# Neuron scan with gated FFN, one core: unread matmuls of block 0 behind the coupling, first weight quarter in three transfers, three low-half parts moved

## The chip, the cores and the metric

One core of one Trainium2 chip runs the whole program. The metric is the device time of one execution in microseconds (us). The engines are named as in the profile: PE is TensorE (PEld its weight loads), DVE VectorE, ACT ScalarE, POOL GpSimd, SP SyncE, which issues most DMAs.

## The reference, cut to what matters

A scan of 128 time steps (T) over 16 batch rows and 256 neurons, each step four Runge-Kutta stages, and on its output a gated mixture-of-experts FFN. Each Runge-Kutta stage needs the one before it.

```python
def _derivative(q, p, drive, coupling, bias):
    i_couple = jnp.tanh(q) @ coupling.T
    dq = q - q ** 3 / 3.0 - p + drive + i_couple + bias
    dp = EPSILON * (q + ALPHA - BETA * p)
# _rk4_step: four derivatives, q and p advanced and clipped; 128 steps in sequence
logits = x @ W_router.T              # x: the q trace, (2048, 256)
sh = _silu_and_mul(x @ Ws_gate_up, I_SH) @ Ws_down
gu = jnp.einsum('th,ehi->eti', x, We_gate_up)      # 8 experts of 176, top 2
out = x0 + shared_out + sparse_out
```

## The kernel before, in words

**Blocks and stages.** The 128 time steps are 16 blocks of 8 steps; a step has 4 stages, so a block has 32 stages (`STAGES`), and the stage number n runs from 0 to 511 over the scan. Block b's FFN is spread over the stages of blocks b+1 and b+2 by tables with one entry per stage. Block 0 (n = 0 to 31) therefore has no FFN work; in it the FFN's weights are prepared instead. After the last block a tail finishes the FFN.

**One stage of the scan.** DVE writes the new q (L907). ACT computes its tanh twice, to f16 (`th_hi`, L475) and to f32 in PSUM (`th_ps`, L476). DVE subtracts them (`th_lo`, L875). PE's `couple` does three 32-column matmuls on the input (L597), eight 16-column matmuls of `th_hi` with the coupling matrix (L613) and four of `th_lo` (L619), all summed in `coup_ps`. DVE then forms the next q from `coup_ps` and its own cubic term (L907).

**What sets the order.** Every engine has one queue in program order, and the orders are written out by hand. On PE a stage is `couple`, then `prepare(n)`, then the `ffn` work of that stage. On DVE the FFN work and the preparation of a stage (`slot`, `prepare`) stand ahead of `th_lo` where the stage is the first of a time step (k = 0), and behind the `force` operation of L886 otherwise.

**Preparing the up weights (block 0 and the start of block 1).** w_up is four quarters of 2112 columns (1056 KB each). In stages n = 1 to 12 ACT sums absolute values of one third of a quarter per stage (L445, 704 columns; part p in stage p + 1), waiting for the quarter's transfer (`in_w`, L444 and after). In stages 13 to 16 these sums become a power-of-two scale: PE turns the column (L543, stage 13) and spreads the maximum (L547, stage 14), each between two DVE steps. From stage 16 on, each of 17 tiles of 4 rows is split in a high f16 half (ACT, `HI_AT`, L453) and a low half. The low half is made in one of three ways: by DVE (`LO_AT`, L830), by POOL in two operations (`POOL_SCALE_AT` L1024, `POOL_LO_AT` L1032), or by PE as two matmuls into a PSUM bank that is free then (`REST_AT`, L577 with an f32 identity, L578), which ACT rounds (`ROUND_AT`, L457). `REST_AT` has two parts in each of stages 18, 19, 22 to 31 and 33, and its first entry is stage 18; tile 4's parts use `up_ps[0]`, in stages 26 and 27.

**Unread matmuls.** In stages 17 to 34 PE also runs matmuls of 128 columns whose result nobody reads (L601). Their number is that of the table `WARM` at n - 1: ten in stages 17, 18, 21 and 22, two in stage 33, none elsewhere (42 in all). They stand inside `couple`, behind the three matmuls of L597 and ahead of the wait for `th_hi`:

```python
WARM_FROM, WARM_TO = 17, STAGES + 3
WARM = [max(0, 10 - 5 * len(REST_AT.get(n, ())) - 8 * (n == STAGES)) for n in range(WARM_TO)]
```

**Loads.** SP issues, in this order: coupling (256 KB), the first 8 steps of x (128 KB), the identity (64 KB), w_up quarters 0 and 1, x steps 8 to 23 (256 KB), w_up quarters 2 and 3, the rest of x, the small constants, w_down (2 MB).

Of the kernel before, what the change touches and what calls it, by code (L numbers as in the profile page):

```python
# [28 lines left out]
P = 128  # L29
# [6 lines left out]
STAGES = 4 * STEPS  # L36
# [36 lines left out]
def err(z):  # L73
# [33 lines left out]
ROWS = 2 * KC  # L107
# [15 lines left out]
            44: ((10, 2, 4),), 47: ((13, 0, 2),), 49: ((13, 2, 4),)}  # L123
REST_BANK = {14: 2, 1: "route", 6: "down", 4: 0, 3: 1, 9: 2, 7: "down", 10: "route", 13: "down"}
LO_AT = {17: (5, 0), 18: (5, 2), 19: (5, 3), 20: (8, 1), 21: (8, 2), 22: (8, 3), 23: (2, 1), 24: (2, 2), 25: (2, 3),
         26: (0, 1), 27: (0, 2), 28: (0, 3), 29: (12, 0), 30: (12, 2), 31: (12, 3), 32: (11, 0), 41: (11, 2),
         45: (11, 3), 48: (15, 0), 49: (15, 3), 52: (16, 1), 55: (16, 2), 56: (16, 3)}
POOL_SCALE_AT = {17: (5, 1), 19: (8, 0), 22: (2, 0), 25: (0, 0), 27: (12, 1), 30: (11, 1), 37: (15, 2), 39: (15, 1),
                 45: (16, 0)}
POOL_LO_AT = {18: (5, 1), 21: (8, 0), 23: (2, 0), 26: (0, 0), 29: (12, 1), 31: (11, 1), 38: (15, 2), 42: (15, 1),  # L130
              46: (16, 0)}


def in_order(table):
# [31 lines left out]
    return max(rounds_done(tile) for tile in REST_TILES if REST_BANK[tile] == bank)  # L166


WARM_FROM, WARM_TO = 17, STAGES + 3
WARM = [max(0, 10 - 5 * len(REST_AT.get(n, ())) - 8 * (n == STAGES)) for n in range(WARM_TO)]  # L170
W_STEPS = 5
HALF = STEPS // 2
X_AHEAD = {1: (0, 2), 2: (0, 3), 3: (1, "m0"), 5: (1, "m1"), 6: (1, 0), 7: (1, 1), 9: (1, 2), 10: (1, 3),
# [9 lines left out]
def program(nc, x, cond, coupling, bias, w_up, w_down, w_route, identity, spread, iota, e_base, out):  # L183
    ctx = ExitStack()
    with ctx:
# [6 lines left out]
        def sem(name):  # L192
            return ctx.enter_context(nc.semaphore(name))
# [86 lines left out]
        in_x_first = sem("in_x_first")  # L280
        in_x_next = sem("in_x_next")
        in_x = sem("in_x")
        in_w = [sem(f"in_w{i}") for i in range(ROWS)]
        in_wd = sem("in_wd")
        setup_v = sem("setup_v")
        setup_t = sem("setup_t")
# [59 lines left out]
        def blocks(block_of):  # L346

            for b in range(BLOCKS):
                block_of(b)
# [10 lines left out]
        @block.sync  # L360
        def _(sync):
            sync.dma_start(cf[:], coupling).then_inc(in_cf, 16)
            sync.dma_start(xs[:, 0:STEPS], x[:, 0:STEPS]).then_inc(in_x_first, 16)
            sync.dma_start(ident[:], identity).then_inc(in_ident, 16)
            for i in range(ROWS):
                sync.dma_start(wf[:, i // 2, i % 2], w_up[:, i // 2, i % 2]).then_inc(in_w[i], 16)
                if i == 1:
                    sync.dma_start(xs[:, STEPS:3 * STEPS], x[:, STEPS:3 * STEPS]).then_inc(in_x_next, 16)
            sync.dma_start(xs[:, 3 * STEPS:T], x[:, 3 * STEPS:T]).then_inc(in_x, 16)
            sync.dma_start(wr[:], w_route).then_inc(in_const, 16)  # L370
            sync.dma_start(iota_s[:], iota).then_inc(in_const, 16)
            sync.dma_start(e_s[:], e_base).then_inc(in_const, 16)
            sync.dma_start(sel[:], spread).then_inc(in_const, 16)
            sync.dma_start(wd[:, 0:TILES - 1, :], w_down[0:(TILES - 1) * P, :].rearrange(
                "(j p) n -> p j n", p=P)).then_inc(in_wd, 16)
            sync.dma_start(wd[0:F % P, TILES - 1, :], w_down[(TILES - 1) * P:F, :]).then_inc(in_wd, 16)

            def store(f):

                sync.wait_ge(out_ready, KC * (f + 1))  # L380
                sync.dma_start(out[:, :, bass.ts(f, TOK)], out_s[:]).then_inc(stored, 16)

            for f in range(BLOCKS):
                store(f)
            sync.wait_ge(stored, 16 * BLOCKS)
# [27 lines left out]
        def _(act):  # L413
# [12 lines left out]
            def prepare(n):  # L426
                if n == 0:

                    nc.scalar.activation(bias_c[:], bias_s[:], ACT.Copy, bias=-SHIFT, scale=1.0).then_inc(setup_a, 1)
                    act.wait_ge(setup_a, 1)  # L430
                    for m in range(KC):
                        bias_x(0, m)

                    act.wait_ge(setup_v, 4)
                    nc.scalar.mul(c16[:, 0, 1], cf[:, 1], scale[:, 0:1]).then_inc(c_cast, 1)
                    act.wait_ge(in_ident, 16)
                    nc.scalar.mul(ident_u[:], ident[:], scale[:, 0:1]).then_inc(unit_cast, 1)

                if SUM_AT <= n < SUM_AT + W_PARTS:

                    part = n - SUM_AT
                    act.wait_ge(in_w[part // 3], 16)
                    if part:
                        act.wait_ge(w_summed, part)  # L444
                    nc.scalar.activation(hidden_flat[:, 0:W_COLS], w_flat[:, bass.ts(part, W_COLS)], ACT.Abs,  # L445
                                         accum_out=w_sum[:, part:part + 1]).then_inc(w_summed, 1)
                if n == MOST_AT:
                    nc.scalar.mul(ident_neg[:], ident[:], -1.0).then_inc(idents_ready, 1)
                for j, r0, r1 in HI_AT.get(n, ()):

                    act.wait_ge(w_scaled, 4)
                    w, w_hi, _ = w_tile(j)
                    nc.scalar.mul(w_hi[:, r0:r1], w[:, r0:r1], scale[:, 1:2]).then_inc(w_hi_ready, 1)  # L453
                for j, r0, r1 in ROUND_AT.get(n, ()):

                    act.wait_ge(w_rest, REST_ORDER.index((j, ROWS - 1)) + 1)
                    nc.scalar.copy(w_tile(j)[2][:, r0:r1],  # L457
                                   rest_bank(j)[:, r0 * P:r1 * P].rearrange("p (r c) -> p r c", r=r1 - r0)
                                   ).then_inc(w_rounded, 1)
                b, st = n // STAGES, n % STAGES  # L460
                for m, at in enumerate(X_AT):
                    if st == at and 2 <= b < BLOCKS - 1:
                        bias_x(b + 1, m)
# [76 lines left out]
        def _(pe):  # L540
# [39 lines left out]
            def couple(b, st):  # L580

                n = b * STAGES + st
                if n == 0:
                    pe.wait_ge(setup_v, 3)
                    pe.wait_ge(unit_cast, 1)
                else:
                    pe.wait_ge(q_ready, n)
                if st % (4 * HALF) == 0:
                    part = 2 + 2 * (st // (4 * HALF))
                    if b < 2:  # L590
                        pe.wait_ge(x_split_ahead, 4 * b + part)
                    else:
                        pe.wait_ge(x_split, 4 * (b - 2) + part)
                t = b * STEPS + st // 4
                at = slice(t, t + 1)
                for x, piece in enumerate((upper(xb, at), upper(x_rest, at), flat(x_low, at))):
                    nc.tensor.matmul(coup_ps[:, 0:CB], ident_u[:], piece, start=x == 0, stop=False,  # L597
                                     skip_group_check=True)
                if WARM_FROM <= n < WARM_TO:
                    for _ in range(WARM[n - 1]):  # L600
                        nc.tensor.matmul(coup_ps[:, 2 * P:3 * P], c16[:, 0, 0, 0:P], c16[:, 0, 0, 0:P],  # L601
                                         start=False, stop=True, skip_group_check=True)

                pe.wait_ge(hi_ready, n + 1)
                if n == 0:
                    pe.wait_ge(setup_v, 6)
                    pe.wait_ge(c_cast, 1)
                for part in range(2):
                    if n == 0 and part:
                        pe.wait_ge(setup_v, 8)  # L610
                    for m in range(KC):
                        for k in range(KC):
                            nc.tensor.matmul(coup_ps[:, m * B:(m + 1) * B], c16[:, part, k, m * P:(m + 1) * P],  # L613
                                             th_hi[:, k, :], start=False, stop=False, skip_group_check=True)

                pe.wait_ge(lo_ready, b * STAGES + st + 1)
                for m in range(KC):
                    for k in range(KC):
                        last = nc.tensor.matmul(coup_ps[:, m * B:(m + 1) * B], c16[:, 0, k, m * P:(m + 1) * P],  # L619
                                                th_lo[:, k, :], start=False, stop=True, skip_group_check=True)  # L620
                last.then_inc(summands, 1)
# [83 lines left out]
            def one_block(b):  # L705
                for st in range(STAGES):
                    couple(b, st)
                    prepare(b * STAGES + st)
                    if b == 1 and st == 0:
                        pe.wait_ge(in_wd, 2 * 16)  # L710
                        pe.wait_ge(in_const, 4 * 16)
                    for f, at in ffn_stages(b, st)[::-1]:
                        ffn(f, at)

            blocks(one_block)
            for f, at in tail_stages():
                ffn(f, at)
# [425 lines left out]
```

## Time and profile before

| what | value |
|---|---|
| median of 3 runs | 653.63 us (652.66, 653.63, 656.25) |
| profiled execution | 656.32 us, of which its span 654.5 us |
| busy in the span | PE 97%, DVE 93%, ACT 55%, POOL 32% |
| chain that ended last | PE 95%, DVE 3%, DMA 1% |
| costliest lines of that chain | L682 29%, L698 22%, L613 17%, L619 15%, L597 6%, L601 1% |
| first and last start of L601 | 28.0 and 54.0 us, 42 matmuls |

The span runs from the first to the last instruction; the execution's own time is 1.82 us longer, for what lies around it. [...] Stage n begins, in what follows, where its first matmul of L597 starts. In the profiled execution stage 2 begins at 8.86 us, stage 17 at 27.93, stage 18 at 29.91, stage 23 at 40.19, stage 27 at 46.67, stage 32 (block 1) at 52.64.

### The profile page before, as it was taken

What the parts mean: (1) busy time and instruction counts of PE and PEld (TensorE: products, weight loads), DVE (VectorE), ACT (ScalarE), POOL (GpSimd) and SP (SyncE); (2) the same over time, 40 slices, a digit from 0 to 9 for tenths busy, and PEclk for the clock granted to TensorE, in tenths of its full rate; (3) what the DMA queues carried; (4) which work ended last, traced back from release to release, by engine and by line L of the source; (5) the groups of instructions that cost most, each with busy time, mean ns of one, the idle gap of its engine ahead of it and who ended that gap; (6) DMA issues with size and microseconds to landing.
All of it is one profiled execution on the core that took longest, in us unless ns stands there. A gap on an engine that the chain in (4) does not pass through costs nothing.

```text
span 654.5 us, 33404 instructions
## 1 busy us (share of the span) xinstructions
PE 637.2 (97%) x12540; PEld 605.6 (93%) x12540; DVE 607.9 (93%) x4517; ACT 359.1 (55%) x1883; POOL 210.3 (32%) x468
## 2 busy tenths in 40 slices
PE   4899999999999999999999999999999999999998
PEld 3699999999999999999999999999999999999997
DVE  7879999999999999999999999999999999999941
ACT  6757655546455554645555564555546455554642
POOL 2214232232423223242322324232232423233253
PEclk9999999999999999999999999999999999999999
DMA  8800000000000000000000000000000000000000
GB/s 331 244 2 3 4 4 11 4 4 11 4 11 4 12 3 4 11 4 12 3 12 3 4 12 3 12 4 12 3 4 12 3 13 3 12 4 3 12 6 15
DMA packets 8786, 13.59 MB, mean 21 GB/s; under 512 B 1168, under 2 KB 7632, under 8 KB 7984
## 3 DMA queue, kind: packets, MB, share of 16 engines
q1 hardware_dynamic: 8336, 11.45, 5.3%
q8 instruction: 98, 1.61, 1.0%
q14 instruction: 64, 0.52, 0.3%
q10 hardware_dynamic: 288, 0.02, 0.0%
HBM read 9.37 MB, written 2.10 MB: 18 GB/s over the span
## 4 chain that ended last, share of the span: by engine, by line
PE 95%; DVE 3%; DMA 1%; ACT 0%; issue 0%; SPq 0%; POOL 0%; DVEq 0%
PE up_ps L682 29%; PE down_ps L698 22%; PE coup_ps L613 17%; PE coup_ps L619 15%; PE coup_ps L597 6%; PE route_ps L657 3%; PE route_ps L636 1%; DMA wf<-in_w_up 1%; PE down_ps L577 1%; PE coup_ps L601 1%; DVE q L907 1%; PE route_ps L577 1%; PE up_ps L577 0%; DVE th_lo L875 0%; DVE w L830 0%
## 5 line engine op out<-in xcount | busy, mean ns | idle before, releaser
L682 PE MATMUL up_ps<-q_hi,w 128*128 128x128 f16 x2176 | 234.8, 218 | 0.2 <-POOL q_lo L1040 0.2
L1077 POOL TENSOR_TENSOR hidden<-hidden,comb_s 128x128 f32<-128x128 f32 x272 | 123.4, 456 | 284.5 <-ACT th_hi L475 278.2
L698 PE MATMUL down_ps<-hidden,wd 128*128 128x128 f32 x1088 | 209.7, 296 | 0.0
L682 PE MATMUL up_ps<-q_lo,w 128*128 128x128 f16 x1088 | 202.8, 218 | 0.0
L475 ACT ACTIVATE th_hi<-q 128x32 f16<-128x32 f32 x384 | 88.0, 229 | 205.4 <-DVE q L907 203.0
L613 PE MATMUL coup_ps<-th_hi,c 128*128 128x16 f16 x4096 | 179.6, 170 | 1.6 <-ACT th_hi L475 0.9
L682 PEld LDWEIGHTS up_ps<-q_hi,w 128*128 128x128 f16 x2176 | 167.6, 97 | 1.0 <-POOL q_lo L1040 0.4
L698 PEld LDWEIGHTS down_ps<-hidden,wd 128*128 128x128 f32 x1088 | 152.9, 191 | 0.0
L613 PEld LDWEIGHTS coup_ps<-th_hi,c 128*128 128x128 f16 x4096 | 139.2, 96 | 9.2 <-ACT th_hi L475 1.0
L619 PE MATMUL coup_ps<-th_lo,c 128*128 128x16 f16 x2048 | 132.7, 173 | 0.3 <-DVE th_lo L875 0.2
L682 PEld LDWEIGHTS up_ps<-q_lo,w 128*128 128x128 f16 x1088 | 105.7, 97 | 0.1
L907 DVE SCALAR_TENSOR_TENSOR q<-coup_ps,c_un,force 128x32 f32<-128x32 f32 x384 | 96.3, 251 | 8.8 <-PE coup_ps L619 5.2
L516 ACT ACTIVATE act_s<-up_ps,unscale 128x128 f32<-128x128 f32 x272 | 97.1, 357 | 8.8 <-PE up_ps L682 8.8
L597 PE MATMUL coup_ps<-xb,ident_u 128*128 128x32 bf16 x512 | 92.7, 181 | 7.9 <-DVE q L907 5.1
L875 DVE TENSOR_TENSOR th_lo<-th_ps,th_hi 128x32 f16<-128x32 f32 x511 | 97.7, 191 | 2.0 <-ACT th_ps L476 1.8
L619 PEld LDWEIGHTS coup_ps<-th_lo,c 128*128 128x128 f16 x2048 | 85.3, 97 | 15.3 <-DVE th_lo L875 0.3
L597 PE MATMUL coup_ps<-x_rest,ident_u 128*128 128x32 bf16 x512 | 90.8, 177 | 0.0
L597 PE MATMUL coup_ps<-x_low,ident_u 128*128 128x32 bf16 x512 | 90.5, 177 | 0.0
L954 DVE TENSOR_TENSOR hidden<-act_s,up_ps 128x128 f32<-128x128 f32 x272 | 76.4, 281 | 13.9 <-ACT act_s L516 13.7
L867 DVE SCALAR_TENSOR_TENSOR square_ps<-q 128x32 f32<-128x32 f32 x384 | 76.8, 200 | 0.0
L871 DVE SCALAR_TENSOR_TENSOR square_ps<-square_ps,q 128x32 f32<-128x32 f32 x384 | 76.4, 199 | 0.0
L739 DVE SCALAR_TENSOR_TENSOR p_sum<-q,p_sum 128x32 f32<-128x32 f32 x384 | 70.8, 184 | 0.0
(122 smaller groups left out, 1060.5 us busy)
## 6 DMA issues: line engine op xcount, KB each, us to landing
wf<-in_w_up SPq DMA_DIRECT2D x4, 1056.0 KB, 10.1
wd<-in_w_down SPq DMA_DIRECT2D x1, 2048.0 KB, 21.2
out<-out_s SPq DMA_DIRECT2D x16, 128.0 KB, 2.2
xs<-in_x SPq DMA_DIRECT2D x1, 1664.0 KB, 18.9
sel<-in_spread SPq DMA_DIRECT2D x1, 408.0 KB, 18.4
cf<-in_coupling SPq DMA_DIRECT2D x1, 256.0 KB, 2.7
xs<-in_x SPq DMA_DIRECT2D x1, 256.0 KB, 9.1
xs<-in_x SPq DMA_DIRECT2D x1, 128.0 KB, 2.7
```

What stands on the lines that cost most here:

```text
L475: nc.scalar.activation(th_hi[:], q[:], ACT.Tanh).then_inc(hi_ready, 1)
L516: nc.scalar.activation(act_s[:, j % 4, :], up_ps[(f * TILES + j) % UPS][:, 0:TOK], ACT.Silu, scale=unscale[:, 1:2]).then_inc(silu_ready, 1)
L597: nc.tensor.matmul(coup_ps[:, 0:CB], ident_u[:], piece, start=x == 0, stop=False, skip_group_check=True)
L613: nc.tensor.matmul(coup_ps[:, m * B:(m + 1) * B], c16[:, part, k, m * P:(m + 1) * P], th_hi[:, k, :], start=False, stop=False, skip_group_ ...
L619: last = nc.tensor.matmul(coup_ps[:, m * B:(m + 1) * B], c16[:, 0, k, m * P:(m + 1) * P], th_lo[:, k, :], start=False, stop=True, skip_gro ...
L682: last = nc.tensor.matmul(up_ps[(f * TILES + j) % UPS][:, h * TOK:(h + 1) * TOK], w16[:, part, k, h, j * P:(j + 1) * P], q[:, k, :], start ...
L698: last = nc.tensor.matmul(down_ps[:, m * TOK:(m + 1) * TOK], wd[:, j, m * P:(m + 1) * P], hidden[:, j, :], start=j == m == 0, stop=j == TI ...
L867: nc.vector.scalar_tensor_tensor(square, q, THIRD[k], q, ALU.mult, ALU.mult).then_inc(squared, 1)
L871: nc.vector.scalar_tensor_tensor(cubic, square, LINEAR[k], q, ALU.subtract, ALU.mult).then_inc(cubed, 1)
L875: nc.vector.tensor_tensor(th_lo[:], th, th_hi[:], ALU.subtract).then_inc(lo_ready, 1)
L907: nc.vector.scalar_tensor_tensor(q_raw[:] if k == 3 else q_in[k + 1][:], coup_ps[:, 0:CB].rearrange("p (m b) -> p m b", m=KC), c_un[:, (0, ...
L1077: nc.gpsimd.tensor_tensor(hidden[:, j, :], hidden[:, j, :], comb_s[:, j, :], ALU.mult).then_inc(weighed, 1)
```

## The change

The loop of unread matmuls leaves `couple` and stands at the end of PE's work of a stage, behind `couple`, `prepare` and `ffn`. It now writes `up_ps[0]` (with start set) in place of a spare part of `coup_ps`. The table gives 8 in each of stages 2 to 17, none in 18 and 19, 10 in 20 and 21, none from 22 on: 148 in all. The first quarter of w_up is loaded in three transfers of 704 columns (352 KB each), each with its own semaphore, and ACT's sums of parts 0, 1 and 2 each wait for one. Three low-half parts move: (11, 0) on DVE from stage 32 to 33; on POOL (15, 1)'s subtraction from 42 to 45, and (16, 0)'s scaling from 45 to 46 and its subtraction from 46 to 47 (the last two are one part).

```diff
--- before.py
+++ after.py
@@ -123,12 +123,12 @@
             44: ((10, 2, 4),), 47: ((13, 0, 2),), 49: ((13, 2, 4),)}
 REST_BANK = {14: 2, 1: "route", 6: "down", 4: 0, 3: 1, 9: 2, 7: "down", 10: "route", 13: "down"}
 LO_AT = {17: (5, 0), 18: (5, 2), 19: (5, 3), 20: (8, 1), 21: (8, 2), 22: (8, 3), 23: (2, 1), 24: (2, 2), 25: (2, 3),
-         26: (0, 1), 27: (0, 2), 28: (0, 3), 29: (12, 0), 30: (12, 2), 31: (12, 3), 32: (11, 0), 41: (11, 2),
+         26: (0, 1), 27: (0, 2), 28: (0, 3), 29: (12, 0), 30: (12, 2), 31: (12, 3), 33: (11, 0), 41: (11, 2),
          45: (11, 3), 48: (15, 0), 49: (15, 3), 52: (16, 1), 55: (16, 2), 56: (16, 3)}
 POOL_SCALE_AT = {17: (5, 1), 19: (8, 0), 22: (2, 0), 25: (0, 0), 27: (12, 1), 30: (11, 1), 37: (15, 2), 39: (15, 1),
-                 45: (16, 0)}
-POOL_LO_AT = {18: (5, 1), 21: (8, 0), 23: (2, 0), 26: (0, 0), 29: (12, 1), 31: (11, 1), 38: (15, 2), 42: (15, 1),
-              46: (16, 0)}
+                 46: (16, 0)}
+POOL_LO_AT = {18: (5, 1), 21: (8, 0), 23: (2, 0), 26: (0, 0), 29: (12, 1), 31: (11, 1), 38: (15, 2), 45: (15, 1),
+              47: (16, 0)}
 
 
 def in_order(table):
@@ -166,8 +166,8 @@
     return max(rounds_done(tile) for tile in REST_TILES if REST_BANK[tile] == bank)
 
 
-WARM_FROM, WARM_TO = 17, STAGES + 3
-WARM = [max(0, 10 - 5 * len(REST_AT.get(n, ())) - 8 * (n == STAGES)) for n in range(WARM_TO)]
+WARM_FROM, WARM_TO = 2, STAGES
+WARM = [8 if n < min(REST_AT) else max(0, 10 - 5 * len(REST_AT.get(n, ()))) for n in range(WARM_TO)]
 W_STEPS = 5
 HALF = STEPS // 2
 X_AHEAD = {1: (0, 2), 2: (0, 3), 3: (1, "m0"), 5: (1, "m1"), 6: (1, 0), 7: (1, 1), 9: (1, 2), 10: (1, 3),
@@ -280,7 +280,7 @@
         in_x_first = sem("in_x_first")
         in_x_next = sem("in_x_next")
         in_x = sem("in_x")
-        in_w = [sem(f"in_w{i}") for i in range(ROWS)]
+        in_w = [sem(f"in_w{i}") for i in range(ROWS + 2)]
         in_wd = sem("in_wd")
         setup_v = sem("setup_v")
         setup_t = sem("setup_t")
@@ -362,8 +362,11 @@
             sync.dma_start(cf[:], coupling).then_inc(in_cf, 16)
             sync.dma_start(xs[:, 0:STEPS], x[:, 0:STEPS]).then_inc(in_x_first, 16)
             sync.dma_start(ident[:], identity).then_inc(in_ident, 16)
-            for i in range(ROWS):
-                sync.dma_start(wf[:, i // 2, i % 2], w_up[:, i // 2, i % 2]).then_inc(in_w[i], 16)
+            for part in range(3):
+                cols = bass.ts(part, W_COLS)
+                sync.dma_start(wf[:, 0, 0, cols], w_up[:, 0, 0, cols]).then_inc(in_w[part], 16)
+            for i in range(1, ROWS):
+                sync.dma_start(wf[:, i // 2, i % 2], w_up[:, i // 2, i % 2]).then_inc(in_w[i + 2], 16)
                 if i == 1:
                     sync.dma_start(xs[:, STEPS:3 * STEPS], x[:, STEPS:3 * STEPS]).then_inc(in_x_next, 16)
             sync.dma_start(xs[:, 3 * STEPS:T], x[:, 3 * STEPS:T]).then_inc(in_x, 16)
@@ -439,7 +442,7 @@
                 if SUM_AT <= n < SUM_AT + W_PARTS:
 
                     part = n - SUM_AT
-                    act.wait_ge(in_w[part // 3], 16)
+                    act.wait_ge(in_w[part if part < 3 else part // 3 + 2], 16)
                     if part:
                         act.wait_ge(w_summed, part)
                     nc.scalar.activation(hidden_flat[:, 0:W_COLS], w_flat[:, bass.ts(part, W_COLS)], ACT.Abs,
@@ -596,11 +599,6 @@
                 for x, piece in enumerate((upper(xb, at), upper(x_rest, at), flat(x_low, at))):
                     nc.tensor.matmul(coup_ps[:, 0:CB], ident_u[:], piece, start=x == 0, stop=False,
                                      skip_group_check=True)
-                if WARM_FROM <= n < WARM_TO:
-                    for _ in range(WARM[n - 1]):
-                        nc.tensor.matmul(coup_ps[:, 2 * P:3 * P], c16[:, 0, 0, 0:P], c16[:, 0, 0, 0:P],
-                                         start=False, stop=True, skip_group_check=True)
-
                 pe.wait_ge(hi_ready, n + 1)
                 if n == 0:
                     pe.wait_ge(setup_v, 6)
@@ -711,7 +709,12 @@
                         pe.wait_ge(in_const, 4 * 16)
                     for f, at in ffn_stages(b, st)[::-1]:
                         ffn(f, at)
-
+                    n = b * STAGES + st
+                    if WARM_FROM <= n < WARM_TO:
+
+                        for _ in range(WARM[n]):
+                            nc.tensor.matmul(up_ps[0][:, 0:P], c16[:, 0, 0, 0:P], c16[:, 0, 0, 0:P], start=True,
+                                             stop=True)
             blocks(one_block)
             for f, at in tail_stages():
                 ffn(f, at)
```

## Rows read from the trace of the kernel before

**Rows 1.** The view by windows: us busy and (x) instructions of each engine, granted clock.

```profile
9.00:26.60 17.60, 12.45 (x214) 9.20 (x212) 14.77 (x113) 14.50 (x56) 4.43 (x9) 1.00 1.04 361
26.60:46.00 19.40, 17.87 (x242) 16.64 (x242) 13.97 (x97) 10.87 (x36) 4.20 (x8) 1.00 0.14 42
46.00:52.60 6.60, 6.60 (x114) 6.26 (x112) 6.42 (x46) 4.83 (x18) 2.06 (x4) 1.00 0.00 0
```

**Rows 2.** The timeline of stages 10 and 11: start, duration, engine, line.

```profile
20.41 0.25 DVE L907 SCALAR_TENSOR_TENSOR q<-coup_ps,c_un,force 128x32 f32<-128x32 f32 x1 [0.16 <-PE coup_ps L619]
...
21.04 0.19 DVE L875 TENSOR_TENSOR th_lo<-th_ps,th_hi 128x32 f16<-128x32 f32 x1
...
21.29 0.27 PE L619 MATMUL coup_ps<-th_lo,c 128*128 128x16 f16 x4
21.61 0.25 DVE L907 SCALAR_TENSOR_TENSOR q_raw<-coup_ps,c_un,force 128x32 f32<-128x32 f32 x1 [0.17 <-PE coup_ps L619]
...
21.91 0.21 PE L597 MATMUL coup_ps<-xb,ident_u 128*128 128x32 bf16 x1 [0.35 <-DVE q_raw L907]
```

**Rows 3.** The timeline of PE, stage 17.

```profile
28.03 1.23 PE L601 MATMUL coup_ps<-c 128*128 128x128 f16 x10
29.05 0.41 PE L613 MATMUL coup_ps<-th_hi,c 128*128 128x16 f16 x8
```

**Rows 4.** The timeline of PE, stage 23 and the start of stage 24.

```profile
40.19 0.23 PE L597 MATMUL coup_ps<-xb,ident_u 128*128 128x32 bf16 x1
...
40.53 0.25 PE L619 MATMUL coup_ps<-th_lo,c 128*128 128x16 f16 x4
40.64 0.77 PE L577 MATMUL route_ps<-wf,ident_w 128*128 128x128 f32 x2
...
41.95 0.23 PE L597 MATMUL coup_ps<-xb,ident_u 128*128 128x32 bf16 x1
```

**Rows 5.** The timeline of PE, stages 26 to 28, and the start of stage 32.

```profile
45.92 0.53 PE L577 MATMUL up_ps<-wf,ident_w 128*128 128x128 f32 x2
...
47.10 0.47 PE L577 MATMUL up_ps<-wf,ident_w 128*128 128x128 f32 x2
...
47.80 0.18 PE L597 MATMUL coup_ps<-xb,ident_u 128*128 128x32 bf16 x1
...
52.64 0.18 PE L597 MATMUL coup_ps<-xb,ident_u 128*128 128x32 bf16 x1
```

**Rows 6.** Line L601 alone, from 27 to 46 us: ns of one, min/median/max.

```profile
L601 PE MATMUL coup_ps<-c x40: 267/314/314, 28.0 to 38.4; 128*128 128x128 f16 x40
```

**Rows 7.** Line L601 alone, from 46 to 60 us.

```profile
L601 PE MATMUL coup_ps<-c x2: 216/216/217, 54.0 to 54.0; 128*128 128x128 f16 x2
```

**Rows 8.** The chain that ended last, a piece of block 1.

```profile
61.12 0.45 PE up_ps L682 x8
```

**Rows 9.** The timeline of ACT, stages 1 and 2.

```profile
7.78 0.18 ACT L476 ACTIVATE th_ps<-q 128x32 f32<-128x32 f32 x1
8.95 0.79 ACT L445 ACTIVATE hidden<-wf 128x704 f32<-128x704 f32 x1 [0.99 <-DMA wf<-in_w_up]
...
9.74 0.21 ACT L475 ACTIVATE th_hi<-q 128x32 f16<-128x32 f32 x1
```

**Rows 10.** The DMA issues up to 2.3 us: count, KB, us from issue to landing.

```profile
wf<-in_w_up SPq DMA_DIRECT2D x1, 1056.0 KB, 6.8
```

**Rows 11.** The DMA issues from 2.8 to 3.3 us (quarter 1, then x).

```profile
wf<-in_w_up SPq DMA_DIRECT2D x1, 1056.0 KB, 8.9
xs<-in_x SPq DMA_DIRECT2D x1, 256.0 KB, 9.1
```

**Rows 12.** The timeline of SP: its issues of quarters 0 and 1.

```profile
2.13 0.91 SPq L366 DMA_DIRECT2D wf<-in_w_up  x2
```

**Rows 13.** The timeline of PE, stage 14.

```profile
25.20 0.58 PE L547 MATMUL route_ps<-most,ones 1*128 1x1 f32 x2
```

**Rows 14.** The timeline of PE, stage 32.

```profile
53.26 0.26 PE L619 MATMUL coup_ps<-th_lo,c 128*128 128x16 f16 x4 [0.18 <-DVE th_lo L875]
```

## Prediction, made before the changed kernel was run

> **What bounds the kernel now.** I read the view by windows first. PE is busy 12.45 of 17.60 us from 9.0 to 26.6, 17.87 of 19.40 up to 46.0, and all of 46.0 to 52.6 [rows 1]. So the two parts of block 0 have different limits. [...]
>
> Then the timeline of an idle stage, 10 to 11. From one L907 to the next it is 21.61 - 20.41 = 1.20 us. The chain goes from q through the tanh to `th_lo` (21.04 + 0.19 = 21.23), L619 (21.29) and L907. PE stands idle 0.35 us before L597 and again before `th_hi` comes [rows 2]. Here the latency of DVE, ACT and PE in turn is the bound, not PE's rate.
>
> From stage 17 PE's queue is the bound. Ten unread matmuls start at 28.03 and L613 at 29.05, so each costs 0.102 us [rows 3], and they stand in front of L613. In a stage with two rest parts, stage 23 runs from 40.19 to 41.95, 1.76 us, of which the parts take 41.95 - 40.64 = 1.31 [rows 4]. With the faster clock the same parts take 47.80 - 47.10 = 0.70, and the four stages 28 to 31 take (52.64 - 47.80) / 4 = 1.21 us each [rows 5]; DVE, 6.42 of 6.60 busy [rows 1], then sets the pace as much as PE.
>
> The last thing to see is ACT in stages 1 and 2. Its first sum of |w_up| waits until 8.95 for the quarter's transfer, though `th_ps` had started at 7.78, and this holds the next tanh until 9.74 [rows 9].
>
> **The change part by part.** I count in starts of stages against the profiled execution.
>
> **1. The first quarter in three transfers.** ACT could start the sum 0.14 us behind `th_ps`, at 7.92, as it does where nothing is missing, and it starts at 8.95 [rows 9]. [...] The sum of stage 1 then ends in time for q of stage 2 (about 8.8), and the tanh that started at 9.74 starts at 8.84: **-0.9 us**. Ends: 0 (the thirds land together at 8.93) and -1.0 (1.03 us of waiting). [...] Two more issues of about 0.45 us [rows 12] delay all later loads' issues by 0.9 us; their cover is the backlog, since quarter 1 lands 8.9 us after its issue [rows 11]. [...]
>
> [...]
>
> **2. Forty unread matmuls leave the front of L613, and with them goes the slow clock.** Stages 17 to 26 run from 27.93 to 46.67, 18.74 us (their starts stand below the table of the profile); 40 x 0.102 = 4.1 us of it are the unread matmuls [rows 3, 6], most of the rest above 1.21 a stage is the slow clock. [...] 10 x 1.21 = 12.1: **-6.6 us**. Ends: 0, and -6.8 at 1.19 a stage. The ten of stages 20 and 21 take 10 x 0.057 = 0.57 behind L619 and fit.
>
> **3. The added matmuls.** In stages 2 to 17 eight stand behind L619. Slow: 0.11 + 8 x 0.102 = 0.93, then L597 0.13 and L613 0.21 [rows 3, 4] give 1.28 a stage against 1.20, so PE becomes the bound by 0.08. Fast: eight such matmuls take 0.45 [rows 8], they end 0.11 + 0.45 = 0.56 behind L619, and the next L597 isn't due before 21.91 - 21.29 = 0.62 [rows 2]. PE's idle time covers them; if it is gone they cost up to 0.45. The profile shows the fall of the durations 18 us after the first unread matmul, but with idle stages between; from stage 2 (9.5 us) on the stream has nearly no gap. I take a rise about 7 us later, after five slow stages: 5 x 0.08 = **+0.4 us**. Ends: 0.1 and 1.3 (all sixteen).
>
> In stages 13 and 14 the eight stand behind PE's turn and spread, which wait for DVE and start at 25.20 in stage 14, over half a stage late [rows 13]. 25.20 + about 0.35 + 0.45 = 26.0, where L597 started at 25.71, less the 0.2 that L597 has in hand: **+0.3 us** for both. Ends 0 and 0.9 (slow clock). The matmuls of `up_ps[0]` collide with no part: tile 4's come in stage 26, the last unread one in 21.
>
> **4. Low parts and stage 33.** In stage 32 L619 waits 0.18 us for `th_lo`, which stood behind the low part of (11, 0) [rows 14]; that goes. In stage 33 the part stands behind `force`, where PE with two rest parts is the bound. The two unread matmuls of stage 33 go, 0.13 us. POOL's moved parts lie beside PE's work, and their tiles are first used some ten stages later; if they cost, it is the 0.43 us of one operation. Together **-0.3 us**; ends 0 and -0.4.
>
> **The sum.** -0.9 - 6.6 + 0.4 + 0.3 - 0.3 = -7.1, and 0.1 for ten fast stages whose matmuls are shorter: -7.2. 656.32 - 7.2 = **649.1 us**. The profiled execution lies 2.7 above the median. The shown runs spread by 3.6 us, and a stage with rest parts costs 1.76 - 1.21 = 0.55 while the clock is slow, so a rise six stages earlier would explain 652.66. The changed kernel has no such stages to lose, so I expect it at 649.1 in all runs, 0.7% under the median. About 0.5% is what a measurement of this kernel can tell from no change: below 650.4 is faster, above 656.9 slower.
>
> **The rivals.**
>
> A. *The profiled execution is high for another reason.* Nothing in the rows says that the other runs differed by the clock. Then the whole gain counts against the median: 653.63 - 7.2 = **646.4**. Faster, too.
>
> B. *The clock rises no earlier.* PE was busy 17.87 of 19.40 us before it rose [rows 1], so eight matmuls a stage may be too thin. Then all sixteen stages pay 0.08 (+1.3), stages 13 and 14 0.5 more than a fast clock, and stages 17 to 22 take 1.28 + 3 x 1.76 + 2 x 1.48 = 9.5 in place of 12.3 (40.19 - 27.93). -0.9 + 1.8 - 2.8 - 0.3 = -2.2: **654.1**, no change. For it: two levels 18 us apart from the first unread matmul. Against it: a slow stage of the new kind is busier than stage 17 was.
>
> C. *The split brings nothing, or costs.* 649.1 + 0.9 = 650.0 if the thirds land together. If each of the two added transfers also delays what is behind it, I bound that by the 0.7 us in which 256 KB followed quarter 1 [rows 11], once each: **650.0 to 651.4**, at the edge of faster. For it: no row shows a small transfer in this place. [...]
>
> D. *Slower: the clock stays low into block 1.* No unread matmuls stand in stages 18, 19 and 22 on. If the clock is still slow when block 1 begins, a stage there with eight matmuls of L682 and two rest parts takes 0.11 + 1.31 + 0.82 + 0.34 = 2.6 in place of 1.2, 1.4 us more. It decides from two such stages on: 654.1 + 2 x 1.4 = 656.9; three give **658.3**. Against it: stages 22 to 31 are as dense as those in which the clock rose before [rows 4].
>
> **How the numbers follow.** The forecast (fast clock well before stage 17) has 0.48, A 0.20, B with risings in between 0.17, C 0.11, D 0.04. Faster: the forecast, A, half of C, a bit of B: 0.75. Same: most of B, half of C, 0.21. Slower: 0.04. The range: A's 646.4 less the ends of part 3 gives 646.0; upward C's 651.4 and a rise only at stage 20 or so give 652.6. B's own value and D lie outside, with less than 2 in 10.
>
> **What would show it.** In the changed profile the first sum of L445 starts at about 7.9, not 8.95. Eight unread matmuls spread 1.0 us at first and 0.6 later, with the fall between stages 5 and 9; their mean is 216 ns from then on. Stages 17 to 31 take 1.21 each, L577 pairs 0.47 us, and stage 32 starts near 45.7. L619 of stage 32 waits for nothing. From stage 33 on the stages keep their lengths. The prediction is wrong where unread matmuls still take 314 ns in stage 17, where a sum waits for a transfer in stages 2 to 4, or where block 0 ends at 46 and the time still isn't below 651.

## The result, and the profile after

The changed kernel takes 649.74 us (median of 11 runs, 649.22 to 651.69), the kernel before in the same comparison 654.25 (11 runs, 651.57 to 659.10). The ratio is 0.9933, 95% interval 0.9910 to 0.9956: 0.7% faster, where 649.1 us was forecast. Single executions that ran in a slower state (724.3 us at a mean clock of 0.67 in run 6, 1653.7 us in run 12, one of the kernel before in each of two groups) are left out of every median here.

The profiled execution of the changed kernel is its slowest, 651.69 us with a span of 649.9, and it shows something that its other runs mostly don't have, going by their times (eight of the eleven lie below 650). A second profile of the same kernel (run `e9_changed_again` below) took 649.34 us, at the median, with a span of 647.5. Both are read here.

The view by windows of the changed kernel, in stretches that follow what happened (columns as in [rows 1]):

```profile
9.00:16.60 7.60, 7.30 (x138) 6.71 (x138) 6.59 (x49) 6.05 (x24) 2.47 (x5) 1.00 1.02 415
16.60:19.20 2.60, 0.29 (x6) 0.14 (x3) 0.18 (x1) 1.03 (x5) 0.00 (x0) 1.00 1.03 432
19.20:25.10 5.90, 5.85 (x113) 5.43 (x113) 5.02 (x39) 5.56 (x22) 1.40 (x3) 0.71 1.04 254
30.00:42.50 12.50, 12.35 (x223) 11.11 (x222) 12.43 (x92) 9.95 (x34) 4.20 (x8) 1.00 0.03 8
42.50:48.50 6.00, 6.00 (x106) 5.64 (x105) 5.93 (x44) 4.62 (x18) 2.06 (x4) 1.00 0.01 3
```

PE is busy from stage 2 on, where it was busy 12.45 of 17.60 us [rows 1]. There is a hole at 16.6, and behind it the granted clock is 0.71 on average. The hole is ACT's, as its timeline shows in stages 1 and 7:

```profile
8.04 0.18 ACT L479 ACTIVATE th_ps<-q 128x32 f32<-128x32 f32 x1
8.16 0.77 ACT L448 ACTIVATE hidden<-wf 128x704 f32<-128x704 f32 x1
...
15.41 0.18 ACT L479 ACTIVATE th_ps<-q 128x32 f32<-128x32 f32 x1
18.17 0.79 ACT L448 ACTIVATE hidden<-wf 128x704 f32<-128x704 f32 x1 [2.57 <-DMA wf<-in_w_up]
```

The first sum starts 0.12 us behind `th_ps` and waits for nothing, where it waited 0.99 us [rows 9]. But the first sum of quarter 2 waits 2.57 us. The DMA issues, by windows of issue time up to 2.5, from 3.5 and from 4.9 us (columns as in [rows 10]), give the landings:

```profile
wf<-in_w_up SPq DMA_DIRECT2D x1, 352.0 KB, 5.1
...
wf<-in_w_up SPq DMA_DIRECT2D x1, 1056.0 KB, 8.3
...
wf<-in_w_up SPq DMA_DIRECT2D x1, 1056.0 KB, 13.5
```

The first third lands at 2.14 + 5.1 = 7.2 us, quarter 1 at 3.56 + 8.3 = 11.9, quarter 2 at 4.64 + 13.5 = 18.1. PE's timeline shows the clock (a row of eight unread matmuls each, and the end of the hole):

```profile
9.83 1.01 PE L716 MATMUL up_ps<-c 128*128 128x128 f16 x8
...
12.38 1.01 PE L716 MATMUL up_ps<-c 128*128 128x128 f16 x8
...
13.63 0.61 PE L716 MATMUL up_ps<-c 128*128 128x128 f16 x8
...
19.23 0.36 PE L611 MATMUL coup_ps<-th_hi,c 128*128 128x16 f16 x8 [2.34 <-ACT th_hi L478]
...
20.88 1.01 PE L716 MATMUL up_ps<-c 128*128 128x128 f16 x8
```

Three stages are slow (1.01 us for eight), from about 13.4 us on they are fast (0.61), and after the hole two and a half are slow again. In the view by windows of one microsecond the fall stands in the granted clock, which before the first rise still read 1.00:

```profile
20.00:21.00 1.00, 0.98 (x22) 0.77 (x20) 0.91 (x8) 1.00 (x5) 0.40 (x1) 0.66 1.14 245
21.00:22.00 1.00, 1.00 (x20) 1.00 (x17) 0.94 (x8) 0.92 (x5) 0.34 (x1) 0.50 0.90 188
```

So the column tells of the lower level (0.50) only once there has been a change; before that the durations have to be read, as in [rows 4 to 7]: the same unread matmul took 314 ns up to 38.4 us and 216 ns at 54.0. The forecast's slow and faster clock are these two levels.

The second profile has no hole in the loads. PE's timeline there:

```profile
12.37 0.93 PE L716 MATMUL up_ps<-c 128*128 128x128 f16 x8
13.56 0.61 PE L716 MATMUL up_ps<-c 128*128 128x128 f16 x8
...
26.64 0.62 PE L716 MATMUL up_ps<-c 128*128 128x128 f16 x8 [0.91 <-issue]
...
30.07 0.47 PE L580 MATMUL up_ps<-wf,ident_w 128*128 128x128 f32 x2
...
46.49 0.18 PE L600 MATMUL coup_ps<-xb,ident_u 128*128 128x32 bf16 x1
46.52 0.18 PE L600 MATMUL coup_ps<-x_rest,ident_u 128*128 128x32 bf16 x1
```

The clock rises at the end of stage 4, at about 13.2 us, and holds; the first rest parts take 0.47 us a pair, where they took 0.77 [rows 4]. Stage 32 starts at 46.49, 6.15 us ahead of 52.64 [rows 5]. The row at 26.64 is new: PE stands 0.91 us with nothing that the profile knows to wait for.

### The profile page after: what moved, and what is told of

It reads as the page before. It is cut to its first block, busy times and chain, and to the rows that moved or that the text cites. A ratio compares the mean times of both kernels' runs of the same rounds, so it can differ in the third digit from the quotient of the medians.

```text
span 649.9 us, 33618 instructions
## 1 busy us (share of the span) xinstructions
PE 636.4 (98%) x12646; PEld 606.2 (93%) x12646; DVE 606.8 (93%) x4517; ACT 359.1 (55%) x1883; POOL 210.3 (32%) x468
## 4 chain that ended last, share of the span: by engine, by line
PE 96%; DMA 2%; DVE 1%; SPq 1%; ACT 0%; issue 0%; POOL 0%; DVEq 0%
PE up_ps L680 29%; PE down_ps L696 22%; PE coup_ps L611 17%; PE coup_ps L617 15%; PE coup_ps L600 5%; PE route_ps L655 3%; DMA wf<-in_w_up 2%; PE route_ps L634 1%; PE up_ps L716 1%; PE up_ps L580 1%; PE down_ps L580 1%; PE route_ps L580 0%; PE route_ps L644 0%; SPq L367 0%; PE up_ps L581 0%
## 5 line engine op out<-in xcount | busy, mean ns | idle before, releaser
L617 PE MATMUL coup_ps<-th_lo,c 128*128 128x16 f16 x2048 | 132.7, 173 | 0.2
L617 PEld LDWEIGHTS coup_ps<-th_lo,c 128*128 128x128 f16 x2048 | 84.9, 96 | 15.7 <-DVE th_lo L878 0.2
L600 PE MATMUL coup_ps<-xb,ident_u 128*128 128x32 bf16 x512 | 92.5, 181 | 2.3 <-ACT ident_u L440 1.4
L600 PE MATMUL coup_ps<-x_rest,ident_u 128*128 128x32 bf16 x512 | 90.7, 177 | 0.0
L600 PE MATMUL coup_ps<-x_low,ident_u 128*128 128x32 bf16 x512 | 90.5, 177 | 0.0
## 6 DMA issues: line engine op xcount, KB each, us to landing
wf<-in_w_up SPq DMA_DIRECT2D x3, 1056.0 KB, 13.5
```

## The experiments

Each run is timed against the kernel before on its own chip. The first four shared 33 runs of it (median 654.28), the next four 23 (654.11), the last four 34 (653.79). Intervals are 95%.

**1. The split alone** (`e1_split_only`): the kernel before, with this part only.

```diff
-            for i in range(ROWS):
-                sync.dma_start(wf[:, i // 2, i % 2], w_up[:, i // 2, i % 2]).then_inc(in_w[i], 16)
+            for part in range(3):
+                cols = bass.ts(part, W_COLS)
+                sync.dma_start(wf[:, 0, 0, cols], w_up[:, 0, 0, cols]).then_inc(in_w[part], 16)
+            for i in range(1, ROWS):
+                sync.dma_start(wf[:, i // 2, i % 2], w_up[:, i // 2, i % 2]).then_inc(in_w[i + 2], 16)
```

> The kernel before with one part of the change: w_up's first quarter in three transfers. Theory (the three transfers take 0.9 us of waiting off stage 2): 0.9 us under before, ratio 0.9986, the first sum starts near 8.2 us in place of 8.95 and waits for nothing. Rival (the split costs what it saves, since later quarters land later): within 0.2 us of before, and a sum further on, the first of quarter 2 in stage 7, waits for its transfer.

654.0 us, ratio 0.9981 (0.9949 to 1.0013). The timing can't tell it from no change. The profile can: stages 1 and 2 take 10.30 - 7.82 = 2.48 us where they took 11.02 - 7.67 = 3.35, and no sum waits for a load. That is 0.87 us, the forecast's 0.9. What the timing scatters by shows PE's timeline of this run, at stage 23:

```profile
39.93 0.75 PE L580 MATMUL route_ps<-wf,ident_w 128*128 128x128 f32 x2
...
40.57 0.44 PE L580 MATMUL route_ps<-wf,ident_w 128*128 128x128 f32 x2
```

The clock rose at about 40.4 us, not at 45.9 as in [rows 5], and the execution took 653.9. The rise moves from profile to profile (45.9, 40.4 and, in run 3, 32.7 us), and the times with it by more than the split can bring.

**2. The change without the split** (`e2_no_split`): the reverse of that diff on the changed kernel.

> The changed kernel with w_up's first quarter in one transfer again. Theory (the unread matmuls' place and number bring most, the split 0.9 us): 0.9 us above the changed kernel and 3.6 to 4.5 us under before. Rival (the split makes the stage-7 wait of the changed kernel's profile, 2.57 us): no slower than the changed kernel, and no run at a granted clock of 0.997.

650.25 us, ratio 0.9913 (0.9879 to 0.9947), 0.5 above the changed kernel's 649.74 (from another comparison) and 4.0 under before. The 0.5 isn't resolved: the two intervals overlap, and the five runs without a recorded dip of the clock (649.26 to 650.26) begin where the changed kernel's do (649.22). The split's 0.9 us shows in the profiles alone, where stage 2 takes 2.45 us here and 1.51 with the split. The rival falls: five of the ten runs have a mean granted clock of 0.997 or less, and the profile has a dip from 29 to 32 us and one more between 200 and 210, without any late quarter 2. The first dip follows 1.18 us in which PE stood still with no releaser, in stage 15.

**3. The moved parts alone** (`e3_low_only`): the kernel before with the changed tables of DVE and POOL.

```diff
-26: (0, 1), 27: (0, 2), 28: (0, 3), 29: (12, 0), 30: (12, 2), 31: (12, 3), 32: (11, 0), 41: (11, 2),
+26: (0, 1), 27: (0, 2), 28: (0, 3), 29: (12, 0), 30: (12, 2), 31: (12, 3), 33: (11, 0), 41: (11, 2),
```

(and (15, 1) from 42 to 45, (16, 0) from 45 and 46 to 46 and 47 on POOL.)

> The kernel before with the three low-half parts moved and nothing else. Theory: 0.1 to 0.2 us under before, since L619 of stage 32 no longer waits 0.18 us for th_lo; nothing that the timing resolves. Rival (stage 33 gets longer by the part's 0.27 us): the start of stage 34 stands where it stood relative to stage 32, 2.62 us later.

657.28 us, ratio 1.0035 (0.9993 to 1.0077), unresolved; its twelve runs spread from 652.3 to 661.3. In the profile stages 32 and 33 take 1.05 + 1.36 = 2.41 us in place of 1.28 + 1.34 = 2.62, so the 0.2 us of `th_lo` are gained there. Half of it is given back in stage 34, which takes 1.37 in place of 1.26. Stage 43 takes 1.19 in place of 1.31: a 128x32 step of DVE (`rest`, L739) took 0.36 us in the profile of before while POOL's subtraction of (15, 1) ran (65.62 to 66.05 us), and takes 0.18 in the same place with POOL idle. The median 3 us above before has no cause in the edit that any row shows. The spread of the clock's rise may carry it, which no run shows. In the profiled run it rose at about 32.7 us, and that run took 652.51:

```profile
31.64 0.74 PE L577 MATMUL up_ps<-wf,ident_w 128*128 128x128 f32 x2
...
32.73 0.53 PE L577 MATMUL up_ps<-wf,ident_w 128*128 128x128 f32 x2
```

**4. Without the early unread matmuls** (`e4_late_only`): only the 20 of stages 20 and 21 stay.

```diff
-WARM = [8 if n < min(REST_AT) else max(0, 10 - 5 * len(REST_AT.get(n, ()))) for n in range(WARM_TO)]
+WARM = [0 if n < min(REST_AT) else max(0, 10 - 5 * len(REST_AT.get(n, ()))) for n in range(WARM_TO)]
```

> The changed kernel without the 128 unread matmuls of stages 2 to 17 (the 20 of stages 20 and 21 stay, behind the coupling). Theory (the early ones pay by raising the clock before the rest parts come): stages 18 to about 24 take 1.76 us with two rest parts at 314 ns a matmul, so 0.55 x 6 = 3.3 us above the changed kernel, about 653. Rival (the gain comes only from taking the 42 from in front of th_hi): the same time as the changed kernel.

651.21 us, ratio 0.9939 (0.9912 to 0.9966). Both fell short. The 128 early ones are worth 1.5 us against 649.74, not 3.3, because the clock didn't wait until stage 24: in the profile it has risen by stage 22. Stages 18 and 19 take 2.02 and 1.76 us, 20 and 21 1.46 and 1.47, then 1.13 and 1.18.

**5. No unread matmuls at all** (`e5_none`): `WARM = [0 ...]` on the changed kernel.

> The changed kernel with no unread matmuls at all. Theory (they pay only through the clock): the clock rises in the rest parts of stages 22 to 31 at the earliest, so six to ten more stages of 1.76 in place of 1.21 us than in the changed kernel, less nothing: 3 to 5 us above it, 653 to 655, and with a wider spread. Rival (what brought the time was only that nothing stands ahead of th_hi): the time of the kernel without the early ones, 651.2, or less.

655.0 us, ratio 1.0012 (0.9987 to 1.0038), the time of the kernel before. The theory holds. With nothing ahead of `th_hi` at all, the kernel is no faster than with forty matmuls there. The reading is that those forty gave back through the clock what they cost in place; only medians bear it out. The clock rises in stage 27 of the profile:

```profile
44.45 0.77 PE L580 MATMUL up_ps<-wf,ident_w 128*128 128x128 f32 x2
45.13 0.47 PE L580 MATMUL up_ps<-wf,ident_w 128*128 128x128 f32 x2
```

**6. The new number at the old place** (`e7_front`): the table of 148, inside `couple`.

```diff
+                if WARM_FROM <= n < WARM_TO:
+                    for _ in range(WARM[n]):
+                        nc.tensor.matmul(coup_ps[:, 2 * P:3 * P], c16[:, 0, 0, 0:P], c16[:, 0, 0, 0:P],
+                                         start=False, stop=True, skip_group_check=True)
                 pe.wait_ge(hi_ready, n + 1)
```

(and the loop at the end of the stage is gone.)

> The changed kernel with its own table of 148 unread matmuls, but at their old place inside the coupling, ahead of the wait for th_hi and into coup_ps. Theory (the place matters as much as the number): a slow stage of stages 2 to 17 takes about 1.8 us (0.27 + 0.55 more), a fast one 1.4 to 1.5, so 5 x 0.5 + 13 x 0.25 = 5.7 us above the changed kernel, about 655. Rival (place is indifferent, since the clock is what pays): within 1 us of the changed kernel.

660.37 us (five runs, 660.03 to 666.25), ratio 1.0133 (1.0093 to 1.0174), 11.1 above the changed kernel on the same chip. The direction of the theory, twice its size. It took a rise at stage 7 for granted, and there was none: PE's timeline has stages of 1.77 us, at the lower clock, up to stage 19.

```profile
14.58 1.01 PE L604 MATMUL coup_ps<-c 128*128 128x128 f16 x8
15.39 0.41 PE L616 MATMUL coup_ps<-th_hi,c 128*128 128x16 f16 x8
15.65 0.25 PE L622 MATMUL coup_ps<-th_lo,c 128*128 128x16 f16 x4
16.25 0.21 PE L600 MATMUL coup_ps<-xb,ident_u 128*128 128x32 bf16 x1 [0.35 <-DVE q L909]
```

Ahead of `th_hi` the same eight lengthen the stage, and the idle 0.35 us in front of L600 stay (PE is busy 8.52 of 10.60 us from 14.48 to 25.08); behind the matmuls of `th_lo` they fill them. The edit also changes where the unread results go (`coup_ps` for `up_ps[0]`); a slow eight takes 1.01 us in either. Place decides twice, by the chain and by the clock.

**7. Half as many** (`e6_four`): 4 in place of 8 in stages 2 to 17.

> The changed kernel with 4 in place of 8 unread matmuls in each of stages 2 to 17. Theory (it takes a nearly unbroken stream to raise the clock): it stays slow through stage 17 and rises in the rest parts, as without the early ones: 651.2 us, stage 18 of 1.9 to 2.0 us. Rival (any steady extra work does it): the clock rises by stage 8 and the median is 649.3 to 649.8, that of the changed kernel.

652.01 us, ratio 0.9967 (0.9942 to 0.9993). In the profile the clock stays slow through stage 21. Stages 13 and 14 cost 1.77 and 1.44 us where they took 1.38 and 1.21, so four bring the cost without the gain. The median is 0.8 us above that of the run with none early, on another chip; those 0.62 us of stages 13 and 14 are most of it.

```profile
20.76 0.59 PE L716 MATMUL up_ps<-c 128*128 128x128 f16 x4
...
30.62 0.74 PE L580 MATMUL up_ps<-wf,ident_w 128*128 128x128 f32 x2
```

**8. Without those of stages 20 and 21** (`e12_early_only`): `WARM = [8 if n < min(REST_AT) else 0 ...]`.

> The changed kernel without the 20 unread matmuls of stages 20 and 21; the 128 early ones stay. Theory (once raised, the clock holds over two stages without them): the same median as the changed kernel, 649.3 to 649.8. Rival (it falls in stages 20 and 21): stages 22 and 23 take 1.76 us and the median is above 650.3.

652.17 us, ratio 0.9985 (0.9953 to 1.0017). The rival holds. PE is busy 3.19 of 4.00 us around stages 20 and 21, and one us later the clock falls for 3.5 us, though PE is fully busy in them (view by windows):

```profile
31.00:35.00 4.00, 3.19 (x61) 2.60 (x58) 3.97 (x29) 3.28 (x11) 1.41 (x3) 1.00 0.03 6
...
36.00:37.00 1.00, 1.00 (x9) 0.94 (x8) 0.97 (x7) 0.76 (x5) 0.03 (x1) 0.51 0.00 0
37.00:38.00 1.00, 1.00 (x19) 0.94 (x19) 0.53 (x6) 0.57 (x1) 0.00 (x0) 0.50 0.00 0
```

Stages 23 and 24 take 1.84 and 1.76 us. All its twelve runs have a mean granted clock of 0.997 or less. The twenty matmuls of stages 20 and 21 are worth 2.4 us (652.17 against 649.74), more than the 128 early ones, and they cost nothing: these stages take 1.03 and 1.22 us without them and 1.06 and 1.21 with them.

**9. x later** (`e8_x_late`): the 256 KB of x behind the last quarter.

```diff
-                if i == 1:
+                if i == ROWS - 1:
                     sync.dma_start(xs[:, STEPS:3 * STEPS], x[:, STEPS:3 * STEPS]).then_inc(in_x_next, 16)
```

> The changed kernel with the 256 KB of x for steps 8 to 23 issued behind w_up's last quarter in place of behind quarter 1, so that quarters 2 and 3 come some 0.6 us earlier. Theory (the upper third of the changed kernel's runs, 650.4 to 651.7, comes from waits for quarter 2 or 3): the median falls by 0.1 to 0.4 us and fewer runs lie above 650.4. Rival (those runs come from dips of the clock that have nothing to do with the loads): the same median and the same share of runs above 650.4.

649.55 us, ratio 0.9937 (0.9913 to 0.9961), with two of seven runs above 650.4, against three of eleven. No difference that these runs can show. The profiled run had no wait for a quarter and yet two dips of the clock, so waits are not the only cause of the upper runs.

**10. The changed kernel again** (`e9_changed_again`), unaltered.

> The changed kernel once more, unaltered, on the same chip as the others of this call. Theory: a median of 649.5 to 650.0, and a profile without the 2.57 us wait for quarter 2, so that its stages 5 to 32 show what the clock alone gives: stage 32 begins near 45.7 us. Rival (the wait belongs to the change): the same wait at stage 7 and stage 32 near 48.5.

649.3 us (12 runs, 648.65 to 652.43), ratio 0.9940 (0.9916 to 0.9964). Its profile is the second one above: no wait for quarter 2, and stage 32 at 46.49 us, 0.8 later than I wrote.

**11. Fewer, wider instructions** (`e10_wide`): 2 matmuls of 512 columns for 8 of 128, in stages 2 to 17, 20 and 21.

```diff
-                            nc.tensor.matmul(up_ps[0][:, 0:P], c16[:, 0, 0, 0:P], c16[:, 0, 0, 0:P], start=True,
-                                             stop=True)
+                            nc.tensor.matmul(up_ps[0][:], c16[:, 0, 0, 0:P], c16[:, 0].rearrange("p k n -> p (k n)"),
+                                             start=True, stop=True)
```

> The changed kernel with its unread work in a quarter of the instructions: 2 matmuls of 512 columns where it had 8 of 128, in stages 2 to 17, 20 and 21 (whole bank up_ps[0]). Theory (columns raise the clock; the unexplained 0.9 us in which PE's queue stood still ahead of stage 15's unread matmuls comes from the number of instructions under the loads): the clock rises between stages 4 and 6 as before, no such gap, 0.3 to 0.9 us under the changed kernel, 648.5 to 649.0. Rival (the gap is not theirs): the gap stays at stage 15 and the median is 649.3 to 649.8.

649.67 us, ratio 0.9939 (0.9913 to 0.9966). The clock rises in stage 5 all the same, with a quarter of the instructions. It saves no time. Its profile has no hole of 0.9 us, and neither has that of run 9, which has the narrow ones; so what makes the hole isn't told by it. What the profile has is a fall of the clock in stage 13, at 23.7 us, and slow stages up to 16.

**12. From stage 0, none in 13 and 14** (`e11_wide_0`): the wide ones, `WARM_FROM = 0`, and 0 for `MOST_AT` and `MOST_AT + 1`.

> The kernel with 2 wide unread matmuls a stage, beginning in stage 0 in place of 2, and none in stages 13 and 14, where they stand behind PE's turn and spread. Theory: stage 13 takes 1.38 in place of 1.62 us, the clock rises one or two stages earlier (0.08 us each): 0.3 to 0.4 us under the wide kernel from stage 2. Rival (two stages without them let the clock fall): stages 15 to 19 are slow, 0.5 to 1.5 us above it.

651.17 us, ratio 0.9947 (0.9919 to 0.9975), 1.5 above the run before it. The rival holds. Stages 13 and 14 take 1.18 and 1.19 us, 0.47 less than with them, and from 26 to 32.9 us the clock is slow: stages 18 and 19 take 1.88 and 1.76. None of its eleven runs has a mean granted clock above 0.997, where six of twelve had with them.

```profile
25.00:26.00 1.00, 0.98 (x17) 0.48 (x14) 0.93 (x9) 0.12 (x3) 0.00 (x0) 1.00 1.11 350
...
27.00:28.00 1.00, 1.00 (x18) 0.58 (x17) 1.00 (x9) 0.87 (x4) 0.47 (x1) 0.50 1.06 340
```

No version beat the changed kernel by more than the runs can tell. The table of the runs by their mean granted clock shows what is left of the spread:

| kernel | runs at 0.999 to 1.000 | runs at 0.996 to 0.997 |
|---|---|---|
| changed kernel, first comparison | 8: 649.22 to 649.91 | 3: 650.45 to 651.69 |
| changed kernel again (10) | 7: 648.65 to 649.34 | 2: 649.81, 649.92 |
| only the late ones (4) | 6: 650.62 to 650.93 | 6: 651.48 to 652.12 |
| four a stage (7) | 6: 650.87 to 651.85 | 6: 652.18 to 653.17 |
| wide (11) | 6: 649.19 to 649.36 | 4: 649.99 to 650.62 |

One recorded dip costs about 0.9 us; without one these kernels repeat within 1 us. Five runs with a lower mean clock (0.992 to 0.995; three of run 10, two of run 11) lie at 650.5 to 652.5.

## Why the prediction was right

The time (649.1 forecast, 649.74 and 649.3 measured) and the mechanism are right: the clock rises well before stage 17, and stages 17 to 26 no longer pay for it. Its "in all runs" is not: three of eleven lie above 650.4, and three of twelve in run 10, all with a mean granted clock of 0.997 or less, dips that it did not have. By its parts, against the second profile:

**Part 1** said -0.9; run 1 shows 0.87 in stages 1 and 2. That the thirds would land one after another was the author's estimate. In the second profile they did, at 2.13 + 5.2 = 7.3, 2.60 + 5.6 = 8.2 and 3.08 + 6.0 = 9.1. The landings as a whole do not keep the order of the issues: in the profile before, 9 KB of constants issued at 5.77 landed at 5.77 + 15.2 = 21.0 us, ahead of the 1664 KB of x, issued at 5.17 and landed at 5.17 + 18.9 = 24.1. The cover named for later loads did not always hold: quarter 1 landed 0.4 later than 2.60 + 8.9 = 11.5 [rows 11, 12] and quarter 2 at 18.1 in place of about 14.8 in one profile, and that cost 2.57 us there. It is not a steady cost: in the ten other profiles of kernels with the split the longest wait for a quarter is 0.6 us. Four of these ten have such a wait for a later quarter (0.19 to 0.60 us), and none of the three profiles without the split. Whether the split makes it likelier stays open. In the timings its 0.9 us was not resolved in either direction (runs 1 and 2).

**Part 2** said -6.6 for stages 17 to 26; they take 40.44 - 27.97 = 12.47 where they took 18.74, -6.3. The 1.21 us of stages 28 to 31 [rows 5] for each of the ten was an estimate that no run shows; they average 1.25. The missing 0.3 lies in stages 17, 18 and 22, which take 1.41, 1.38 and 1.35 us in place of 1.21, less what stage 20 saves with 1.06. In stage 17 DVE makes the scaled identity and a low part in one stage, and the 1.41 stand in the kernels without unread matmuls ahead of it too (runs 4 and 5).

**Part 3** had the mechanism and two wrong sizes. Slow stages do take 1.28 (from L617 of stage 2 to that of stage 3), but three of them and not five: the rise came some 3.4 us after the first unread matmul, where I had taken 7. In run 8, with the same table up to there, it came after 5.8 us and five slow stages, so both happen. And the three cost nothing. From the `th_lo` matmuls of stage 2 to those of stage 5 it is 3.77 us here (9.68 to 13.45) and 3.77 in run 1 (9.60 to 13.37), which has no unread matmul there: stages 2 and 3 take 1.28 anyway. Stages 2 to 12 take 13.26 us in place of run 1's 13.39, so -0.1 where the forecast had +0.4 and -0.1. Stages 13 and 14 take 2.84 in place of 2.59, +0.25 for the forecast's +0.3. What the step did not have is PE's hole of 0.91 us ahead of stage 15's unread matmuls. Stages 15 and 16 take 2.76 there in place of 2.22, +0.54.

**Part 4** said -0.3: stages 32 to 43 are 0.21 shorter (14.66 for 14.87). More than half of that is stage 43 (1.19 for 1.31), which it did not have; the `th_lo` wait goes, but stage 34 is 0.16 longer, and the two unread matmuls of stage 33 bring nothing (1.36 us with them in run 3, 1.36 without).

The sum up to stage 32 is -6.15 with a start that was 0.25 later, and 0.6 more comes bit by bit over the other fifteen blocks, 0.04 a block; in the first profile of the changed kernel it is 0.02 and less. The 0.64 between the two profiles lies mostly in the two executions themselves: from stage 44 to the end they take 586.99 and 586.35 us, and all other profiles without a dip of the clock there 586.41 to 586.85, the first one of the changed kernel 586.70. So the near hit of the profiled time (649.34 for 649.1) is partly luck. Block 0 gave 6.4 where the forecast had 6.9, the start was 0.25 later, and 0.55 more than forecast came behind stage 32, nearly all of it where nothing had been changed.

**The rivals.** A, that the profiled execution of before was high for another reason, falls. Three profiles with the forty matmuls in their old place (before, and runs 1 and 3 with one small part of the change each) have the rise at 45.9, 40.4 and 32.7 us and take 656.3, 653.9 and 652.5 us. A changed kernel near 646 never occurred. B, no earlier rise, is what run 7 shows with half as many, at 652.0, and not what this change does. C fell with the landing at 7.2, as far as it had the thirds land together; that the split delays what is behind it is open, as said. D is in no profile: even the kernel without any unread matmuls had risen by stage 27. But four executions of the kernel before and four of run 3 took 660.6 to 661.3 us. A rise at the start of block 1 would give some 656.3 + 6 x 0.55 = 659.6 (an estimate from the profile before), so in these the clock may have been slow into block 1. No run of the changed kernel was above 652.43.

The part that the prediction undersold is the twenty matmuls of stages 20 and 21. I let them "fit" and gave them no worth. Without them more than half of the gain is gone (run 8).

## What to carry to other kernels

Unread matmuls paid here only where PE would have stood idle anyway: behind the last matmul that others wait for, not ahead of the wait for an operand; against none at all (655.0) the same 148 bring 5.7 us in the one place (649.3) and cost 5.4 in the other (660.4), all on one chip. Here they had to close every thin stretch up to the dense work: two stages left open lost the clock for stages that are busy themselves (stages 23 and 24 took 1.84 and 1.76 us in run 8, 18 and 19 took 1.88 and 1.76 in run 12), and four a stage in place of eight cost without bringing anything (run 7). Where single executions scatter by more than the effect, find the time at which the durations change in several profiles before comparing medians.

## What the runs showed of the hardware

In the changed kernel's first profile the granted clock in the windows reads 1.00 before its first recorded change even while matmuls run at the lower level (eight unread matmuls 1.01 us at 9.83 against 0.61 at 13.63, both under a column of 1.00). The duration of a known matmul, 314 or 216 ns [rows 6, 7], is the safer witness. In a row these durations overlap: ten of up to 314 ns stand in 1.23 us [rows 3, 6], so what one adds is the distance between starts, 0.102 us there.

Dips also come where PE had been fully busy. In run 4 the clock fell in the midst of block 1, and stages 33 to 35 took 4.91 us in place of 3.95:

```profile
46.00:49.00 3.00, 3.00 (x53) 2.83 (x50) 2.90 (x22) 2.08 (x10) 0.62 (x2) 1.00 0.00 0
49.00:52.50 3.50, 3.49 (x50) 3.21 (x50) 3.10 (x26) 2.45 (x11) 0.85 (x2) 0.61 0.03 7
```

Runs 5, 8, 9, 11 and 12 have one at the same place, 49 to 55 us, and runs 2 and 3 have one between 200 and 210 us, behind 5 us in which PE was busy throughout. The changed kernel's two profiles have neither. What sets them off is open.

PE's holes without a releaser (0.91 us in the second profile, 1.18 in run 2, 0.65 in run 8) all stand in stage 15 in front of the unread matmuls, at 25 to 28 us, where the weights' loads still run (347 GB/s in the mean from 12.4 to 28 us). In the second profile the view of the DMA queues has no packet of an instruction queue from 24 to 28 us, and in run 2 the last ones lie between 24 and 26 us, ahead of its hole (26.7 to 27.9). So that view shows no transfer of that kind beside the holes. No run here took the loads away, and the cause stays open.
